# Attention over graph edges: the masked maximum starts from the running maximum, which ScalarE carries from strip to strip

## What is computed

```python
for i in range(L):
    Q = _ln(h @ Wq[i], gq[i], bq[i])
    K = _ln(h @ Wk[i], gk[i], bk[i])
    qi = Q[src]; kj = K[dst]
    score = (qi * kj).sum(-1) + 0.1 * (edge_attr * qi[:, :RBF]).sum(-1) + logm[dst]
    smax = jax.ops.segment_max(score, src, num_segments=N)
    es = jnp.exp(jnp.minimum(score - smax[src], 20.0))
    denom = jax.ops.segment_sum(es, src, num_segments=N)
    alpha = es / (denom[src] + 1e-10)
    m = h[dst] @ Wm[i]
    aggi = jax.ops.segment_sum(alpha[:, None] * m, src, num_segments=N)
    # then a linear layer on [h, aggi], a leaky ReLU, a residual and a layer norm
```

## Time and profile before

| what | value |
|---|---|
| median of 3 runs | 14422.83 us |
| the profiled execution, its own time | 14439.23 us |
| its span in the trace | 14436.2 us |
| attention strips (4 x 260) | 1040 |
| busy share of the span: TensorE, VectorE, ScalarE, GpSimd | 83%, 84%, 56%, 46% |
| mean granted TensorE clock over the span | 0.72 of full |

### The profile page before, as it was taken

The page is one execution under the profiler, slowest core; times in us unless marked ns, Lnnn a source line. Parts: engine busy times, 40 slices in busy tenths (PEclk is TensorE's granted clock), DMA queues, the critical chain, the costliest instruction groups (busy, mean ns, idle before and its releaser), DMA issues.

```text
span 14436.2 us, 629801 instructions
## 1 busy us (share of the span) xinstructions
PE 12006.1 (83%) x196113; PEld 10166.6 (70%) x196114; DVE 12152.6 (84%) x30027; ACT 8150.1 (56%) x25978; POOL 6611.7 (46%) x7657
## 2 busy tenths in 40 slices
PE   2899999976776899979997999989996767587666
PEld 2666666765665878878887888878886666576656
DVE  5788888767888989988998899888997789688897
ACT  0344444245666688857886788868884212067630
POOL 0566666634443544435442544344441355564336
PEclk9999999998855955576555855585555578685587
DMA  9322222475898788848884888768887966589957
GB/s 380 96 60 60 60 60 60 50 163 200 282 312 248 292 224 224 224 182 268 224 224 141 309 224 223 192 243 243 227 226 229 321 201 222 137 307 312 283 186 204
DMA packets 3472104, 3003.68 MB, mean 208 GB/s; under 512 B 2332483, under 2 KB 2809876, under 8 KB 3471750
## 3 DMA queue, kind: packets, MB, share of 16 engines
q1 hardware_dynamic: 2746678, 1318.56, 34.0%
q0 software_dynamic: 236192, 860.68, 20.6%
q10 hardware_dynamic: 489008, 821.78, 15.3%
HBM read 1855.14 MB, written 1144.89 MB: 208 GB/s over the span
## 4 chain that ended last, share of the span: by engine, by line
PE 37%; DMA 18%; DVE 15%; issue 10%; SPq 9%; ACT 7%; DVEq 2%; ACTq 1%; POOL 1%; POOLq 0%
DMA chunk_layer_rows<-arena 7%; PE ps L1264 6%; PE ps L1124 5%; PE ps L1298 5%; PE ps L1115 5%; PE ps L1284 4%; DVE arena L1849 4%; SPq L617 3%; DMA arena<-edge_hot_b 3%; DMA chunk_rows<-arena 3%; ACT arena L985 2%; PE ps L1232 2%; PE ps L1107 2%; ACT arena L819 2%; DMA chunk_gated<-arena 2%
## 5 line engine op out<-in xcount | busy, mean ns | idle before, releaser
L1232 PE MATMUL ps<-block_tables,arena 128*128 128x98 bf16 (+2 forms) x56160 | 2480.1, 202 | 638.5 <-DVE arena L1762 330.7
L1264 PE MATMUL ps<-arena 128*128 128x49 bf16 x56160 | 2585.4, 213 | 499.2 <-DVE arena L1792 260.3
L1264 PEld LDWEIGHTS ps<-arena 128*128 128x128 fp8e4 x56160 | 2324.5, 115 | 798.2 <-issue 780.9
L1232 PEld LDWEIGHTS ps<-block_tables,arena 128*128 128x128 bf16 x56160 | 2251.0, 100 | 868.0 <-ACT arena L923 337.0
L737 POOL COPY block_tables<-arena 128x294 bf16 (+2 forms) x2340 | 1429.2, 611 | 2337.8 <-PE ps L1232 1359.0
L923 ACT ACTIVATE arena<-ps 128x392 f32<-128x392 f32 (+1 forms) x3900 | 1711.4, 480 | 1126.8 <-PE ps L1232 582.9
L699 POOL DMA_INDIRECT edge_records<-arena x1563 | 1554.6, 995 | 1233.2 <-DVE arena L1541 841.6
L985 ACT ACTIVATE arena<-arena,small 128x49 f32<-128x49 f32 x8320 | 1997.3, 323 | 100.4
L721 POOL DMA_INDIRECT arena<-chunk_layer_rows,map_a x1040 | 997.4, 959 | 1780.7 <-ACT arena L985 1689.2
L1762 DVE TENSOR_SCALAR arena<-arena,iota_row 128x1024 bf16<-128x1024 uint8 x2080 | 1563.4, 752 | 117.0 <-PE ps L1232 75.2
L1849 DVE CUSTOM_DVE_ANT_0 arena<-ps,arena 128x1024 bf16<-128x1024 f32 x1040 | 1273.2, 1224 | 342.4 <-PE ps L1298 241.8
(11 more groups left out here) (322 smaller groups left out, 20050.6 us busy)
## 6 DMA issues: line engine op xcount, KB each, us to landing
arena<-node_hot_a SPq DMA_DIRECT2D x1820, 256.0 KB
chunk_layer_rows<-arena ACTq DMA_DIRECT2D x1040, 392.0 KB, 3.3
arena<-edge_hot_a SPq DMA_DIRECT2D x1560, 128.0 KB
chunk_gated<-arena ACTq DMA_DIRECT2D x520, 324.0 KB, 2.8
arena<-edge_records SPq DMA_DIRECT2D x1040, 160.0 KB
chunk_rows<-arena ACTq DMA_DIRECT2D x780, 196.0 KB, 1.9
arena<-edge_records SPq DMA_DIRECT2D x520, 196.0 KB
arena<-edge_hot_b SPq DMA_DIRECT2D x780, 128.0 KB
```

The lines of the kernel that those rows point to most:

```text
L1232: last = pe.matmul(psv[:, 2 * r + j // tpb, (j % tpb) * w:(j % tpb + 1) * w], ht4[:, s, j * P:(j + 1) * P], bt4[:, s, i, 0:w], start=i == ...
L1264: last = pe.matmul(to[s % 2], he4j[:, s % 4, j, :], low_part(i, s, j), start=j == 0 and i == 0, stop=j == C8 - 1 and i == 2)
```

## The change

ScalarE gets the column `old`, minus infinity's stand-in or the previous strip's running maximum: `prior(k)` computes old = (maximum after strip k-1) + new_block[k], where the new table `new_block` is 0 if strip k belongs to the same block as strip k-1 and -1e30 if not. `peak` takes `old` as the first value of its maximum, instead of -1e30, and writes the new running maximum straight into `mx3`. `raised` and `kept` go, and with them `nneg`; `low` goes from VectorE to ScalarE; the sign of the maximum turns, so `shifted` subtracts. ScalarE's order per turn becomes weights(t-2), weigh(t-2), low(t-1), prior(t), corrected(t-1), masks(t), turn(t); VectorE's becomes shifted(t-2), products(t), peak(t-1), reduced(t), middles(t), once(t-2), twice(t-2), add_raised(t-3). ScalarE no longer reads the block's number, VectorE reads it once a turn and no longer twice. `new_block` is built once, by a matmul on a larger `ones` and four VectorE instructions of 260 columns or fewer.

```diff
-                def corrected(k, s, b):
-                    hold(act, "act", (at["max"], base + k + 1))
-                    act.activation(cor[:, s % 4:s % 4 + 1], nneg[:, bass.ds(b, 1)], ACT.Exp, bias=mx3[:, s % 2, 0:1], scale=-1.0).then_inc(at["cor"], 1)
-
-                def kept(k, s, b):
-                    hold(act, "act", (at["cor"], 2 * base + 2 * k + 1))
-                    act.activation(nneg[:, bass.ds(b, 1)], mx3[:, s % 2, 0:1], ACT.Copy).then_inc(at["cor"], 1)
+                def low(k, s):
+                    r = s % 2
+                    act.wait_ge(at["gm"], base + k + 1)
+                    act.activation(mx3[:, r, 1:2], mxh[:, r, 0, 1:2], ACT.Identity, bias=mx3[:, r, 0:1], scale=-1.0).then_inc(at["low"], 1)
+
+                def prior(k, s):
+                    r = s % 2
+                    if isinstance(k, int) and k == 0:
+                        act.activation(old[:, 0:1], neg_big[:, 0:1], ACT.Copy).then_inc(at["old"], 1)
+                    else:
+                        hold(act, "act", (at["gm"], base + k))
+                        act.activation(old[:, r:r + 1], mx3[:, 1 - r, 0:1], ACT.Identity, bias=new_block[:, bass.ds(k, 1)]).then_inc(at["old"], 1)
+
+                def corrected(k, s):
+                    r = s % 2
+                    hold(act, "act", (at["gm"], base + k + 1))
+                    act.activation(cor[:, s % 4:s % 4 + 1], mx3[:, r, 0:1], ACT.Exp, bias=old[:, r:r + 1], scale=-1.0).then_inc(at["cor"], 1)
...
-                walk(nc, act, NS, [(2, weights), (2, weigh), (1, READ), (0, masks), (1, corrected, True), (0, turn), (1, kept, True)], (ACT_ENGINE, blk_a))
+                walk(nc, act, NS, [(2, weights), (2, weigh), (1, low), (0, prior), (1, corrected), (0, masks), (0, turn)])
...
                 def peak(k, s):
                     r = s % 2
-                    hold(dve, "dve", (at["bc"], base + k + 1), (at["not"], base + k + 1))
-                    dve.tensor_tensor_reduce(out=junk[:, :], in0=ps[:, 4 * 512:6 * 512], in1=hn4[:, s % 4, :],
-                                             scale=1.0, scalar=-BIG, op0=ALU.add, op1=ALU.max, accum_out=gm[:, r:r + 1]).then_inc(at["gm"], 1)
-
-                def raised(k, s, b):
-
-                    r = s % 2
-                    dve.wait_ge(at["gm"], base + k + 1)
-                    wait(dve, at["cor"], 2 * base + 2 * k)
-                    dve.scalar_tensor_tensor(mx3[:, r, 0:1], gm[:, r:r + 1], -1.0, nneg[:, bass.ds(b, 1)], ALU.mult, ALU.min).then_inc(at["max"], 1)
-
-                def low(k, s):
-                    r = s % 2
-                    dve.wait_ge(at["max"], base + k + 1)
-                    dve.tensor_tensor(mx3[:, r, 1:2], mx3[:, r, 0:1], mxh[:, r, 0, 1:2], ALU.subtract).then_inc(at["low"], 1)
+                    hold(dve, "dve", (at["bc"], base + k + 1), (at["not"], base + k + 1), (at["old"], base + k + 1))
+                    dve.tensor_tensor_reduce(out=junk[:, :], in0=ps[:, 4 * 512:6 * 512], in1=hn4[:, s % 4, :], scale=1.0,
+                                             scalar=old[:, r:r + 1], op0=ALU.add, op1=ALU.max, accum_out=mx3[:, r, 0:1]).then_inc(at["gm"], 1)
...
-                    dve.tensor_tensor(dif[:, r * C8:(r + 1) * C8], sc4[:, s % 4, 0:C8], psv[:, 6, 0:C8], ALU.add).then_inc(at["sub"], 1)
+                    dve.tensor_tensor(dif[:, r * C8:(r + 1) * C8], sc4[:, s % 4, 0:C8], psv[:, 6, 0:C8], ALU.subtract).then_inc(at["sub"], 1)
...
-                    dve.wait_ge(at["cor"], 2 * base + 2 * k + 1)
+                    dve.wait_ge(at["cor"], base + k + 1)
...
-                walk(nc, dve, NS, [(2, shifted), (0, products), (1, READ), (1, peak), (0, reduced), (1, raised, True), (0, middles), (1, low),
+                walk(nc, dve, NS, [(2, shifted), (0, products), (1, peak), (0, reduced), (0, middles),
                                    (2, once), (3, READ), (2, twice), (3, add_raised, True)], (DVE_ENGINE, blk_a))
...
+                if n == 0:
+                    pe.matmul(psv[:, 5, 0:NS], ones[0:NB, :], sels[0:NB, 0:NS], start=True, stop=True)
...
+                if n == 0:
+                    of = sel_f[:, NS:2 * NS]
+                    do(dve.tensor_scalar(of, psv[:, 5, 0:NS], float(NB - 1), None, ALU.min))
+                    do(dve.memset(new_block[:, 0:1], -BIG))
+                    do(dve.tensor_tensor(new_block[:, 1:NS], of[:, 1:NS], of[:, 0:NS - 1], ALU.is_equal))
+                    do(dve.tensor_scalar(new_block[:, 1:NS], new_block[:, 1:NS], BIG, -BIG, ALU.mult, ALU.add))
...
-                do(dve.memset(nneg[:, :], BIG))
```

More of the change, by code:

```diff
@@ L57 @@
 BT = P * C8
-LAYER_CHAIN = 168
+LAYER_CHAIN = 167
 PARAMS = 7 + 6 + 2 + 3 + 2 * 9 + 1
@@ L209, in build @@
         ztype = sb("node_type", [P, NB], I32)
-        nneg = sb("node_max_negative", [P, NB])
+        new_block = sb("new_block", [P, NS])
         scr = sb("score_ring", [P, 4 * 2 * C8])
@@ L221, in build @@
         cor = small[:, 4:8]
-        gm = small[:, 32:34]
+        old = small[:, 32:34]
         lg = small[:, 40:40 + 2 * C8]
@@ L236, in build @@
         iop = sb("iota_row", [P, 1])
-        ones = sb("ones", [P, 1])
+        ones = sb("ones", [P, P])
         sel = sb("select_row", [2 * C8, C8 * P], BF16)
@@ L413, in build @@
         at = {n: sem("att_" + n) for n in (
-            "q", "keys", "not", "prod", "red", "mid", "tr", "ev", "bc", "gm", "max", "low", "cor",
+            "q", "keys", "not", "prod", "red", "mid", "tr", "ev", "bc", "gm", "old", "low", "cor",
             "sub", "exp", "ph")}
```

## The result

The changed kernel takes 14963.72 us (median of 4 runs, 14957.05 to 14970.96), the kernel before 14423.69 us beside it: ratio 1.0374, 95% interval 1.0356 to 1.0392, slower by 540 us. Forecast were 14970 us and a range of 14670 to 15270. A second measurement gave 14964.47 against 14429.72 us, 1.0372 (1.0355 to 1.0389). The profiled execution took 14958.24 us, 519 more than that of before.

What follows compares the result with a forecast made beforehand. A two-strip loop through three engines set 4.234 us per strip; the change closes a one-strip loop whose terms sum to 4.76 us. Over 1040 strips that adds 547 us, giving 14970 us against 14422.8, range 14670 to 15270.

Steps and rivals of the forecast that it cites:

- two-strip loop: Rival: `peak` to next-but-one `peak`, 8.52 us before, still decides and grows to 8.95, 4.475 per strip, 14675 us; chance 8%.
- The new loop: Loop over one strip, `peak(t-1)` through ScalarE's `low`, `masks`, `turn` and TensorE's `spread_s` to `peak(t)`: 4.76 us (4.52 to 5.05).
- `peak` with the scalar and its readout: VectorE's `peak` with accumulator read, 1.23 us, plus 0.06 for a per-partition scalar in place of a constant.
- to ScalarE: Handover from VectorE's `peak` to ScalarE's `low`: 0.10 us, taken between 0.04 and 0.12.
- three short operations: ScalarE's `low`, `prior` and `corrected` ahead of `masks`: 3 x 0.20 = 0.60 us (0.57 to 0.84).
- to the next `peak`: From `spread_s`'s end to VectorE's `peak`: 0.31 us with two holds, plus 0.09 for a third hold on `old`.
- the base: Old period per strip, 4.234 us, read from 260 `peak`s of the fourth round and applied to all 1040 strips.
- in time for `low`: ScalarE finishes `weigh` 0.8 us into the next strip, before the maximum arrives at 1.33; `low` idles some 0.5 us a strip.
- TensorE's share: TensorE's busy share in attention should fall from 97.7% to about 87%.
- The clock: Rival: TensorE gets its higher clock in attention, `spread_s` falls by up to 0.5 us, no change, 14440 us; chance 5%.
- VectorE's list: Rival: VectorE's own instructions set the period, two fewer save 0.24 us a strip, -250 us, 14170 us; chance 7%.
- The distance of 0.19 between short activations: Rule for ScalarE: `low` and `prior`, with bias columns, take 0.19 us each, making the estimate some 30 us lower.

Runs made afterwards that it cites:

- experiment 3: Changed kernel with `peak`'s three holds reordered so that the one on `spread_s` comes last: 15588.93 us, 1.0068 of the kernel before.
- experiment 2: Changed kernel with `masks(t)` moved ahead of `low(t-1)` on ScalarE, run twice: 15608.45 us (1.0090 of the kernel before), then 14643.28 us (1.0156).
- the first set: Four runs (`masks` behind `corrected` on the kernel before; changed kernel with `masks` first, `spread_s` hold last, or one operation more) beside the kernel before at 15464.37 us.

## Why the prediction was right, step by step

**The unit and the bound.** That a two-strip loop set the old period is borne out by the exchanged holds: 57 us forecast from it, 53 measured, and 114 if the loop had been one strip long.

**The new loop.** Its terms, as predicted and as the fourth round shows them: `peak` with the scalar and its readout 1.29 and 1.29 (1284 ns against 1224); to ScalarE 0.10 and 0.04; three short operations 0.60 and 0.57; `masks` 1.04 and 1.04; `turn` 0.30 and 0.31; `spread_s` 1.03 and 1.03; to the next `peak` 0.40 and 0.43. Sum 4.76 and 4.71. That `masks` behind the wait is what hurts is shown twice: the order alone costs the old kernel 615 us, and undoing it in the new one gives back 321.

**What was mis-sized.** Terms of the loop and the base, which nearly cancelled. The way from VectorE to ScalarE was too long by 0.06 and the three operations by 0.03; the way into `peak` was too short by 0.03, because a met hold costs 0.11 and not 0.09 (half of the 0.23 of experiment 3), and `turn` by 0.01. The sum was 0.05 too long for the fourth round. The base, 4.234, was read from the fourth round alone; the mean of all rounds is 4.275. And the changed kernel has 4.81 in the first three rounds, where the sequencer adds 0.09 between `low` and `prior`, which no row of the fourth round could show. Forecast were 0.526 us per strip more, measured 0.508. The closeness of the total, 14970 to 14964, is partly luck: with the right base, 4.275, and the changed kernel's true period in round four, 4.712, for all rounds, the forecast would have been 0.437 x 1040 = 454 us.

**Covers.** ScalarE was in time for `low` (idle 0.41, forecast about 0.5); `weights` waits 0.15 us a strip, a third of what it did, where I had written that the wait should nearly vanish; `spread_s` waits 0.43 for `turn` (about 0.5 forecast); TensorE's share fell to 88% (87 forecast). VectorE's came out at 80.2%, where I had written below 80. The clock stayed at 0.50, so that rival had no case.

**The rivals.** VectorE's list did not decide: two instructions fewer on it, and the kernel is slower. The Trainium skill (VectorE: DVE Perf Modes, Rules for kernel authors) says of chained VectorE operations to minimise their count; this trace speaks against using that alone, since VectorE waited 0.32 us a strip before `peak` already, and now waits 0.86. The two-strip loop lay where it was put, 4.49 forecast in experiment 2 and 4.498 and 4.453 measured, only hidden under the longer one; a second way of the same length, through `low` and `pick_max`, ran beside it, which the prediction's rival did not have. The distance of 0.19 between short activations held in the fourth round: 0.20, 0.19 and 0.18 with lengths of 0.28 to 0.29. The Trainium skill (ScalarE: Activation LUTs, What ACT_TABLE_LOAD costs) has about 280 ns with a bias column and an overlap of about 93 ns, and this trace agrees; the first distance in the other rounds, 0.29, is the sequencer's.

## What to carry to other kernels

Before moving an operation behind a wait in an in-order queue, write down what stands behind it in that queue and whom that work feeds: the 1.04 us of `masks`, which needed nothing of the wait, cost 321 us here and 615 us on the old kernel. An idea should be judged apart from its place: the kernel with the carried maximum lost 3.7% in one order and gained 0.9% in another, of which 0.4% came from the exchange of holds. And in a list of waits with increments ahead of one instruction, put the one that is met last at the end: each one behind it cost 0.10 to 0.12 us on the path here.

## What the runs showed that I had not expected

Sequencer time is visible right after a wait: `prior` starts 0.29 us after `low` in the three rounds inside the loop and 0.20 in the one outside it, and an extra operation costs 0.09 in the former and 0.19 in the latter.

In the first set the kernel before took 15464 us, 7% more than in the others, with `peak` at 1284 ns in both runs of experiment 2. Most of it lies outside the attention strips. The two traces of experiment 2 differ by 962 us: 583 ahead of the first `peak` (5642.1 against 5058.9), 268 behind the last one, and 111 between them. The kernels bound by a one-strip loop had the same period in both sets, the one with masks first 4.61 against 4.50. In its trace the waits of `pick_max` are put down to issue and no longer to `low`, and `spread_s` waits for `turn`. These lines are from the first set, 10700 to 11400 us:

```profile
PEld ps L1321 <- issue: 39.3, 138, 0.5
...
PEld ps L1310 <- ACT scores_turned L963: 25.4, 119, 0.3
```

What makes issue slower there stays open; the kernel before was not profiled in that set.

TensorE's granted clock stayed at 0.50 (1.2 GHz) in attention even when it was 99.2% busy, while the window of a spread stage in the earlier trace rows has 1.00 with 96.5%. What decides between the two levels is not shown here.
